# Moving the folded output weight, a network's answers, the last tiles and the column sums in a two-layer graph-transformer kernel

## The reference

```python
def reference(x, src, dst, edge_weight, ...):
    xn = layernorm(x)
    # layer 0: normalised graph convolution and linear attention
    deg = segment_sum(ew, dst); dinv = where(deg > 0, rsqrt(deg), 0)
    gnn = segment_sum((xn @ W)[src] * (dinv[src] * ew * dinv[dst])[:, None], dst) + b
    q, k, v = heads(xn @ w_qkv)                  # 8 heads of 64
    q, k = elu(q) + 1, elu(k) + 1
    kv = k^T v;  z = 1 / (q . sum(k) + 1e-6)     # per head
    x = x + gnn + (q kv * z) @ w_out + b_out
    # a 7-layer network of 160 units, two positions for each node
    h = one row for each node and position, from 5 features of layernorm(x)
    for i in range(7): h = h @ W[i].T + b[i]     # relu after all but the last
    res = clip(round(h[..., RESULT]), 0, 15)
    x = x + layernorm(x) with 2 * one_hot(res) * mask added to features 128 to 159
    # layer 1: low-rank graph layer and softmax attention
    xn = layernorm(x)
    gnn = relu(segment_sum(((xn @ U * s) @ Vt)[src] * ew[:, None], dst) + bias)
    q = softmax(q, features of a head); k = softmax(elu(k) + 1, over nodes)
    x = x + gnn + (q (k^T v)) @ w_proj + b_proj
    # Haar transform, a small MLP on its low band, inverse transform
    return x + haar_mlp(layernorm(x))
```

## Time and profile before

| what | us |
|---|---|
| median of 3 runs (lowest, highest) | 639.48 (638.75, 640.98) |
| the profiled execution | 642.34 |
| its span, first to last instruction | 640.6 |
| PE busy | 570.3 |
| DVE busy | 478.9 |
| ACT busy | 328.4 |
| POOL busy | 259.0 |

### The profile page before, as it was taken

The page is one execution under the profiler, slowest core; times in us unless marked ns, Lnnn a source line. Parts: engine busy times, 40 slices in busy tenths (PEclk is TensorE's granted clock), DMA queues, the critical chain, the costliest instruction groups (busy, mean ns, idle before and its releaser), DMA issues.

```text
span 640.6 us, 8669 instructions
## 1 busy us (share of the span) xinstructions
PE 570.3 (89%) x2939; PEld 460.1 (72%) x2939; DVE 478.9 (75%) x1044; ACT 328.4 (51%) x619; POOL 259.0 (40%) x290
## 2 busy tenths in 40 slices
PE   3988899989999798999999939998979997998976
PEld 2767787667778586888776627777867886686866
DVE  7689998979996777578968766666765555677764
ACT  7867886767656612122147534445346774323161
POOL 4747776756787215346716920004010221022020
PEclk9999999999999898999999969998999997999979
DMA  9300000000010201113040200000020000110004
GB/s 316 123 2 1 1 1 2 2 1 1 2 67 2 65 0 34 34 36 74 13 140 3 65 0 1 1 0 2 0 83 0 1 1 1 36 49 0 1 4 158
DMA packets 15045, 21.11 MB, mean 33 GB/s; under 512 B 3260, under 2 KB 6000, under 8 KB 15002
## 3 DMA queue, kind: packets, MB, share of 16 engines
q1 hardware_dynamic: 13674, 17.94, 8.9%
q10 hardware_dynamic: 1328, 2.62, 1.2%
HBM read 18.00 MB, written 2.56 MB: 32 GB/s over the span
## 4 chain that ended last, share of the span: by engine, by line
PE 58%; DVE 21%; ACT 6%; issue 6%; POOL 4%; DMA 3%; DVEq 1%; SPq 1%; ACTq 0%; POOLq 0%
PE p L2050 6%; PE p L1887 4%; PE p L2168 4%; PE pQ L2168 4%; PE pQ L1903 3%; PE pH L1903 3%; DVE onehot L1294 3%; PE p L2285 2%; PE p L2135 2%; PE pKV L2135 2%; PE pQ L2347 2%; PE pH L2062 2%; PE p L1903 1%; PE pKV L1932 1%; DMA nodes<-in_x 1%
## 5 line engine op out<-in xcount | busy, mean ns | idle before, releaser
L973 POOL TENSOR_TENSOR Loh<-onehot,whl 128x512 fp32r<-128x512 f32 x85 | 89.4, 1052 | 47.7 <-DVE onehot L1294 47.7
L1294 DVE TENSOR_SCALAR onehot<-iota_src,srclo 128x128 fp32r<-128x128 f32 x170 | 74.8, 480 | 0.7 <-DVE flagint L1306 0.7
L2050 PE MATMUL p<-G,ATs 128*128 128x512 f32 x300 | 73.5, 402 | 0.0
L1887 PEld LDWEIGHTS p<-Roh,Loh 128*128 128x128 f32 x340 | 47.6, 190 | 31.6 <-issue 27.7
L2050 PEld LDWEIGHTS p<-G,ATs 128*128 128x128 f32 x300 | 57.7, 194 | 12.7 <-issue 0.7
L1887 PE MATMUL p<-Roh,Loh 128*128 128x200 f32 x340 | 53.2, 279 | 11.8 <-POOL Loh L973 4.6
L564 ACT ACTIVATE away<-iota_key,key 128x200 f32<-128x200 f32 x85 | 38.8, 456 | 24.3 <-PE p L1887 24.2
L1903 PE MATMUL pQ<-wsl,xT 128*128 128x512 f32 x168 | 47.4, 411 | 2.4 <-DVE xT L1208 2.4
L1903 PE MATMUL pH<-wsl,xT 128*128 128x512 f32 x168 | 45.4, 397 | 0.0
L1145 POOL TENSOR_TENSOR xT<-xn,xT 128x512 fp32r<-128x512 f32 x10 | 12.9, 1288 | 74.7 <-ACT xT L795 74.3
L991 POOL TENSOR_TENSOR ATs<-AT,ATs 128x1280 fp32r<-128x1280 f32 x10 | 29.5, 2950 | 29.7 <-ACT ATs L624 29.4
(11 more groups left out here) (629 smaller groups left out, 1448.8 us busy)
## 6 DMA issues: line engine op xcount, KB each, us to landing
xb<-in_x SPq DMA_DIRECT2D x9, 256.0 KB, 2.7
out<-nodes SPq DMA_DIRECT2D x9, 256.0 KB
wraw<-in_L_mix_w_qkv ACTq DMA_DIRECT2D x2, 1024.0 KB, 7.8
raw<-in_L_mix_w_qkv SPq DMA_DIRECT2D x2, 1024.0 KB, 5.1
nodes<-in_x SPq DMA_DIRECT2D x1, 1024.0 KB, 9.1
wraw<-in_L_mix_w_qkv SPq DMA_DIRECT2D x1, 1024.0 KB, 11.4
wraw<-in_L_gnn_W SPq DMA_DIRECT2D x1, 1024.0 KB, 13.6
raw<-in_L_mix_w_out SPq DMA_DIRECT2D x1, 1024.0 KB, 5.2
```

Source lines behind the costliest of these rows:

```text
L973: pool.tensor_tensor(Loh[:, g % SLOTS], o, w, ALU.mult).then_inc(S["oh_pool"], 1)
L1294: ins = v.tensor_scalar(onehot_[:, g % SLOTS, c, :], iota_src[:], srclo[:, 2 * g + c:2 * g + c + 1], None, ALU.is_equal)
L1887: ins = pe.matmul(pW[g % 2][:, 0:T * WIN], Loh[:, g % SLOTS, c, part, :], Roh[:, g % RSLOTS, c, :], start=(c + part == 0), stop=(c + part ...
L2050: ins = pe.matmul(pG[u][:, :], ATs[:, u, x, s_, :], G[:, y, s_, :], start=(s_ + n == 0), stop=(s_ == T - 1 and n == 2))
```

## The change

It has four parts. **A:** the folded products go ahead of, between and (one of them) behind the degree products and the last query product, in the order `MORDER` 0, 1, 3, 2; the key sums are spread last, into pA, and `q_scaled` reads them there (tile 9 from a copy made at tile 5); the splits of the folded weights go ahead of the degrees and into the G loop, `q_scaled(0)` goes behind g_lo(7), and POOL's bias rows wait for it. **B:** the answers lie in PSUM behind the network's rows, `answers` and `ln_coefficients` are cut in two, layers 20 to 23 stand ahead of the first turn and 24 behind it, in the loop the transposed tile's copy stands ahead of the exponential, and the second group's steps stand in the middle of tiles 2, 3 and 4; Wv's split waits for the second norm's coefficients. **C:** the loop ends at tile 7; tiles 8 and 9 are written out, with keys ahead of queries and the maxima between. **D:** the column sums stand at tile 9's place ahead of steps 22 and 23. Line numbers below L2000 shift by 19 to 49 in the new file, those of the tensor block by 80 to 103.

The diff, cut to its core (where ACT, DVE and PE change in the same way, one of them stands):

```diff
-BESIDE_Q = ((24,), (28,)) + ((),) * (T - 2)
+BESIDE_Q = ((), (28,)) + ((),) * (T - 2)
+MORDER = (0, 1, 3, 2)
...
@@ scalar, A @@
             q_out(T - 2, et, pKV[0])
-            act.wait_ge(S["ksb_ps"], 1)
-            act.activation(xn[:, 0, :], pH[:, :], ACT.Copy).then_inc(S["ksb_ok"], 1)
+            m_hi(0)
+            m_hi(1)
             act.wait_ge(S["deg_ok"], 1)
             act.activation(dinv[:], small[:, 0, :], ACT.Sqrt).then_inc(S["deg_sqrt"], 1)
+            m_hi(3)
             for t in range(T):
                 if t == T // 2:
                     q_out(T - 1, et, pT)
+                    m_hi(2)
                 act.activation(G[:, 0, t, :], nodes[:, t, :], ACT.Copy, scale=dinv[:, t:t + 1]).then_inc(S["g_hi"], 1)
             qt_hi(0)
-            for p, bank in enumerate(mbank):
-                act.activation(WO[:, 0, p, :], bank[:, :], ACT.Copy).then_inc(S["m_hi"], 1)
...
@@ gpsimd @@
             pool.wait_ge(S["b_ld"], 32)
+            pool.wait_ge(S["qs_ok"], 1)
             pool.tensor_tensor(brow[:, 0, :], brow[:, 0, :], brow[:, 1, :], ALU.add).then_inc(S["bias_ok"], 1)
...
-            pool.wait_ge(S["x2_ok"], 2)
+            pool.wait_ge(S["ln_ok"], 6)
             for c in range(KC):
                 ins = pool.tensor_copy(Wv[:, 0, c], raw[:, c])
...
@@ vector, A @@
-                step(v.tensor_tensor(et[:], qv, xn[:, 0, :], ALU.mult))
+                if t == 5:
+                    v.tensor_copy(xn[:, 0, :], pA[:, :]).then_inc(S["ksb_ok"], 1)
+                step(v.tensor_tensor(et[:], qv, pA[:, :] if t < T - 1 else xn[:, 0, :], ALU.mult))
...
+            for t in range(5):
+                g_lo(t)
+            q_elu(T - 1, et, pT)
+            m_lo(2)
+            for t in range(5, 8):
+                g_lo(t)
+            v.wait_ge(S["ksb_ps"], 1)
+            q_scaled(0)
+            g_lo(8)
+            g_lo(9)
             qt_lo(0)
             q_scaled(1)
+            step(aggregated(0))
             qt_lo(1)
             q_scaled(2)
-            step(aggregated(0))
...
@@ vector, B @@
+                rs = rbank[g][:, 64:64 + 2 * n].rearrange("p (t q) -> p t q", q=2)
-                h = oneh[:, 0:n, :]
+            def answered(g):
+                h = rbank[g][:, 128:128 + 32 * n].rearrange("p (t j) -> p t j", j=32)
...
+            def new_roots(g):
+                ln_roots(5 + g, t0, t1, rbank[g][:, 96:96 + t1 - t0])
...
+            for t in range(T - 2):
+                first_sub(t)
+                xt1_lo(t + 1, (t + 1) % 2)
                 if t == 2:
                     answers(1)
+                    answered(1)
                 if t == 3:
                     new_coefficients(1)
+                if t == 4:
+                    new_roots(1)
+                first_elu(t)
+                first_sum(t)
+                first_u(t)
...
@@ vector, D (called at t == T - 1 of the keys' loop, ahead of a2_lo(22), a2_lo(23)) @@
+            def column_sums():
+                v.wait_ge(S["z_one"], T + after["z_one"])
                 step(v.tensor_tensor(diag, pKV[0][:, :].rearrange("p (c n) -> p c n", c=KC),
                                      ident[:].rearrange("p (c n) -> p c n", c=1).broadcast_to([P, KC, P]), ALU.mult))
...
@@ tensor @@
+            for k in range(20, 24):
+                layer(k)
             turn(0, 0, True)
-            for k in range(21, 24):
-                layer(k)
+            layer(24)
...
+            first_k(T - 2, last_turn)
+            first_u(T - 2)
+            first_k(T - 1)
+            first_q(T - 2)
...
+            pe.wait_ge(S["kmax_ok"], T)
+            for c in range(KC):
+                ins = pe.transpose(pKV[0][:, c * P:(c + 1) * P], kmax[:, c * P:(c + 1) * P], ident[:])
+            first_u(T - 1)
             turn_weights(0)
             turn_weights(1)
...
+            first_q(T - 1)
             turn_weights(2)
             low_rank(0)
```

330 lines of the change are left out of this document (187 added, 143 removed).

## The result

| | before | changed |
|---|---|---|
| median, us (4 runs each) | 640.21 | 615.52 |
| lowest to highest | 638.75 to 640.98 | 614.79 to 615.90 |
| profiled execution, its span | 642.34, 640.6 | 614.79, 613.0 |
| mean granted clock in it | 0.968 | 0.983 |

The changed kernel is 24.7 us faster: ratio 0.9616, 95% interval 0.9593 to 0.9638. The prediction was 610.0 us in a range of 604.0 to 619.5. The gain is 83% of the 29.6 us forecast.

The account below looks back on a forecast made before the run. TensorE's own sequence was taken as the bound, with idle stretches and half clock to win back. Terms 8.2 + 9.7 + 3.1 + 5.2 + 3.4 = 29.6 us, off the median 639.48, gave 610 us, range 604 to 619.5.

Parts of the forecast that it names:

- A, to agg(2): From the first G product to the third tile's G products: reordered scaled queries shorten PE's waits, gaining 4.1 us.
- A, to agg(3): Third to fourth tile's G products: q_scaled(3) reads PSUM, so POOL's delay, PE's wait and the clock fall go; 4.1 us.
- B1: Network's answers and first turn (365 to 401 us): PSUM answers and layers ahead of the turn gain 9.7 us, bounds 8 to 10.5.
- B2: Second group of answers (420 to 440 us): cut into three tiles' slots, gain 3.1 us after 2.5 of collisions; bounds 0, 5.6.
- C: Last tiles (460 to 485 us): keys first, maxima and exponentials under other products; gain 5.2 us, bounds 3.5 and 6.5.
- D: Column sums (533 to 554 us): put first, they shorten PE's wait and the clock need not fall; 3.4 us (2 to 4).
- R1: Rival: POOL's Wv split and bias rows hit DVE harder at tile 4 and q_scaled(1); gain 23, 616.5 us; 22%.
- R3: Rival: a PSUM operand doesn't free a DVE operation from POOL; gain 20.6, 619 us; 8%.
- R4: Rival: gaps between layers 20 to 23 drop the clock, which stays at 1.2 GHz to q(5); slower, 645 us; 2%.

Follow-up runs that it names:

- keysum_sbuf: Changed kernel with q_scaled reading the key sums from SBUF, copied once from pA at tile 0: median 619.58 us, ratio 0.9692 to before.
- answers_sbuf: Changed kernel with answers, one-hot rows and the Newton steps' scratch in SBUF again, order as changed: median 617.37 us, ratio 0.9640 to before.
- no_c: Changed kernel with the last tiles as before (loop over all ten, keys behind queries): median 616.92 us, ratio 0.9626 to before.
- d_fill: Changed kernel plus five throwaway matmuls, three ahead of Z's transposes, two ahead of the product with Wv: median 611.87 us, ratio 0.9578 to before.
- no_a: Changed kernel with folded products, key sums, scaled queries and POOL's bias rows as before: median 618.62 us, ratio 0.9642 to before.

## Why the prediction was right, and where it was off

Step by step, from the two profiled executions:

| step | forecast | measured | how |
|---|---|---|---|
| A, to agg(2) | 4.1 | 5.0 | 240.59 to 235.56 |
| A, to agg(3) | 4.1 | 3.9 | 254.96 to 245.99, less the 5.0 |
| between | 0 | 1.3 | L2087 no longer waits for POOL |
| B1 | 9.7 | 9.8 | 400.80 to 380.75, less what stands above |
| B2 | 3.1 | 5.0 | 5.6 by q(5), 0.6 lost again by q(7) (453.69 to 428.66) |
| C | 5.2 | 4.6 | 484.83 to 455.20, less what stands above |
| D | 3.4 | -0.2 | 553.29 to 523.91, less what stands above |
| the rest | 0 | -1.8 | 87.3 to 89.1 from Wp on |
| sum | 29.6 | 27.6 | 642.34 to 614.79 |

The steps' net miss is 2.0 us, but it is made of 6.0 lost (D, the rest, C) and 4.0 gained (B2, between, A, B1). That the number came so near is in part luck.

**A** came by its own steps. Its 8.9 us hold the 0.7 by which the first G product began later in this execution (213.57 against 212.88); counted from there it is 9.7. q_scaled(0) was ready in time, q_scaled(1) ended at 229.2 instead of 230.5, since POOL beside it cost DVE 0.2 us and not 1.4 (L1439 took 0.36), so PE waited 1.34 and not 2.4. (POOL cost 1.0 us more just ahead, at g_lo(8) and g_lo(9), 2.44 us for the two against 1.41 before; q_scaled(0) had ended 0.6 us early, at 223.4.) L1437 was 0.67 us long at 240.09 with L1009 running: reading PSUM frees it, and keysum_sbuf shows the price of not doing it (2.33). What the sum left out is L2087, where PE had waited 1.08 us for POOL's small copies. Their last ends at 302.5 instead of 312.8, 10.3 us earlier, while PE had become 9.0 earlier. With A undone the wait is back (1.11), so A removed it; by which of POOL's instructions isn't settled. I had asked only what POOL does to DVE, never when POOL is done itself.

**B1** was right to 0.1, and by its own steps: the turn came at 365.89, which with the 10.2 us gained ahead of it is 376.1 against 376.2 forecast. There were gaps of 0.67, 0.46 and 0.92 us ahead of layers 21 to 23, none ahead of the turn, and no fall of the clock. answers_sbuf shows that the PSUM half of this part is worth 4.2 of the 9.8 us, half clock included; the order wasn't undone by itself.

**B2** was mis-sized by the price of Wv's split. The collision happened as described (L1716 1.14 and L1718 1.24 us for 0.2 each, L1704 0.98 for 0.69), but 2.2 us on DVE became 0.45 us of waiting on PE and 0.6 us of delay, not 2.5: tile 4 had more slack than I gave it. q(3) to q(5) took 13.7 us, where the prediction had about 16. So R1, with 22%, was wrong in its mechanism although its 616.5 us lies next to the measured time. L1716 and L1718 each ended 0.1 us behind a single piece of POOL's row; L1625 in answers_sbuf waited across several. The Trainium skill, page "SBUF — State Buffer", section "Who interferes with whom", says that the second to come waits to the end of the other's instruction: the first two agree, the third doesn't.

**C** was 0.6 short of the forecast, within its bounds, and needed the waits it was to remove: they return in no_c.

**D** is the term that failed, and in one step of its working: "the clock then need not fall to 0.76". The waits did what the text says (2.98 to 0.75), the clock at the transposes stayed up, and a later fall took the product with Wv instead, 3.8 us. Where it doesn't fall, D is worth 68.4 - 65.0 = 3.4 us, which is the forecast. The sum reckoned the clock as something that waits take away and that better cover gives back. The runs show that it can also fall behind gaps of 0.75 and 0.49 us, in three of nine kernels that had them, and that undoing a part far ahead can change whether it does; what decides stays open.

**The rest** was put at nothing, as the code there is the same, and cost 1.8 us. 1.6 of them lie behind the wait of 2.94 us: from the transposes behind it (557.98, before 587.37) to the product with MW at 580.60 (before 608.39) it is 22.6 us, 21.0 before, and the first product of this stretch took 4.46 us, 2.99 before. The clock fell behind this wait now (558 to 562) and not before, the same thing as in D.

**The scale** is the larger part of the miss in the gain (29.6 forecast, 24.7 between the medians). The forecast put the gain on the median of before. But the profiled execution of before was 2.1 us over the median of its kind and that of the changed kernel 0.7 under, so 27.6 us between the profiles are 24.7 between the medians. The prediction named the 2.9 us between the profile and its median, and took it that the gain carries over whole. What made these 2.9 us isn't shown: among the other runs of before one of 637.8 us had the same mean clock of 0.968 as the profiled one of 642.3.

R3 (PSUM doesn't free an operation) is refuted by L1624, L1437 and the two experiments on them. The trace of before could have settled its doubt whether L1457 ever met POOL: four of its ten ran wholly beside L991 (at 252.84, for one, with L991 running from 252.66 for 2.93 us), and took 0.75 us. R4 (slower) found no sign: the clock was 1.00 through the layers.

## What to carry to other kernels

Cut every trace at marks and compare the pieces; three of these experiments cost 4 to 5 us where the edit was and gave back 4 us a hundred microseconds later, so that their totals alone (0.4 to 1.9 us above the changed kernel's first median) would have said that the edits were worth next to nothing. Where VectorE stands on the critical path beside GpSimd, try a PSUM operand for its small operations: here it made 0.18 us of 2.98. And where TensorE must wait on a path that is otherwise its own, throwaway matmuls into a bank that is free can keep its clock up: twenty-five of them in the waits of 2.94 and 3.7 us brought the last stage from 88.0 us (d_fill) to 86.0. The kernel with all thirty and a small change on GpSimd is 7 us faster than the changed one, but 3.7 of them lie in the product with Wv, where the filling isn't shown to be the cause.

## What was not expected of the hardware

- Sixteen throwaway matmuls (3.7 us of TensorE) in the way of everything behind cost no time, because a fall of the clock that cost as much didn't come (613.4 us of span against 613.0 and 613.5).
- The clock can fall while TensorE is at work: in the changed kernel it went to 0.50 at 510.5 us with TensorE busy 0.95 us of that microsecond, some 2 us behind a gap of 0.49 us, and stayed there for 10 us of unbroken small matmuls. Before, it had stayed at 1.00 while TensorE worked 0.62 of 2 us, and in no_a through a wait of 2.50 us. Which gap brings a fall could not be told from the traces.
- A 128x12 operation of VectorE in SBUF waited 2.8 us for a row of GpSimd instructions, twice to the hundredth of a microsecond the same (2.98 in before and in answers_sbuf), over the ends of several of them; one with 128x512 operands (2.33 us in keysum_sbuf) got in at the end of the first.
